# Loads of weight slices that wait one step less, and quantizing two tiles at a time in the first half of a stage

## What is computed

```
x = x + attn(layernorm(x))
x = x + ffn(layernorm(x))

attn: q, k, v = x Wq^T, x Wk^T, x Wv^T     (8 query heads, 2 kv heads, of 256)
      rope on q and k; unit layernorm of q (times 256), k, v per head
      scores q k^T / 16, causal window of 512, 30 tanh(s / 30), softmax, times v, times Wo^T

ffn:  h = relu(bitlinear(x, w1))^2         (w1 is 8192 x 2048)
      y = bitlinear(h, w2)                 (w2 is 2048 x 8192)
bitlinear(x, w): w_scale = 1 / mean|w|;      w_q = clip(round(w * w_scale), -1, 1) / w_scale
                 x_scale = 127 / max|x| per token; x_q = clip(round(x * x_scale), -128, 127) / x_scale
                 return x_q w_q^T
```

## Time and profile before

| | us |
|---|---|
| runs | 7140.6 and 7159.1, median 7149.9 |
| the profiled execution | 7127.2 |
| its span on the slowest core | 7125.6 |
| spans of the 8 cores | 7056.1 to 7125.6 |

### The profile page before, as it was taken

How to read it: one execution, slowest core, us unless ns; L and a number is a source line. 1 busy time by engine, 2 the same in 40 slices (tenths; PEclk the granted TensorE clock), 3 DMA queues, 4 the chain that set the end, 5 groups by cost and what they waited for, 6 DMA issues and landing times.

```text
span 7125.6 us, 37166 instructions; the slowest of 8 cores (7056.1 to 7125.6 us)
## 1 busy us (share of the span) xinstructions
PE 3207.2 (45%) x12168; PEld 1280.3 (18%) x12168; DVE 2700.4 (38%) x2542; ACT 1311.1 (18%) x1432; POOL 372.3 (5%) x516
## 2 busy tenths in 40 slices
PE   0153254243435253166665555551454644655543
PEld 0021022111112111022222222220221211222211
DVE  2233335243444445233334444443443533433312
ACT  1232332221213040233333333321000000000000
POOL 1000000000000000000000000000000000000000
PEclk9676677676768677588888777775777877877776
DMA  8333331402020201655554444433577777777766
GB/s 178 124 112 112 113 99 37 83 30 59 15 68 6 67 11 50 139 165 165 165 165 145 161 154 157 145 133 127 153 169 157 152 141 144 152 152 156 158 183 194
DMA packets 447711, 872.30 MB, mean 122 GB/s; under 512 B 280608, under 2 KB 301088, under 8 KB 393760
## 3 DMA queue, kind: packets, MB, share of 16 engines
q0 software_dynamic: 81920, 457.21, 26.2%
q1 hardware_dynamic: 232480, 379.16, 16.5%
q10 hardware_dynamic: 133120, 33.56, 3.4%
HBM read 491.29 MB, written 334.50 MB: 116 GB/s over the span
## 4 chain that ended last, share of the span: by engine, by line
DMA 38%; DVE 21%; ACT 11%; PE 8%; ACTq 8%; issue 6%; SPq 4%; DVEq 4%; POOLq 0%; PEldq 0%
DMA yacc_hbm<-arena_f 13%; DMA h_hbm<-arena_f 5%; ACTq L186 5%; DMA arena_f<-w2T 4%; DVEq L212 4%; SPq L186 4%; DMA arena_f<-w1T 4%; DVE arena_f L1118 3%; DMA arena_f<-x_tm 3%; PE ps_o L777 3%; ACTq L212 3%; DMA w2q_hbm<-arena_bf 2%; DMA arena_f<-h_hbm 2%; DMA arena_f<-x_hbm 2%; ACT arena_bf L927 2%
## 5 line engine op out<-in xcount | busy, mean ns | idle before, releaser
L1106 PE MATMUL ps<-arena_bf 128*128 128x512 bf16 x4096 | 1071.1, 428 | 1148.4 <-DMA arena_bf<-hq_hbm 683.9
L996 PE MATMUL ps_f<-arena_bf 128*128 128x512 bf16 x4096 | 1102.9, 437 | 891.0 <-DVE arena_f L1003 735.6
L1106 PEld LDWEIGHTS ps<-arena_bf 128*128 128x128 bf16 x4096 | 433.8, 108 | 1785.7 <-issue 1426.4
L996 PEld LDWEIGHTS ps_f<-arena_bf 128*128 128x128 bf16 x4096 | 438.7, 109 | 1554.7 <-issue 1215.3
L1118 DVE COPY arena_f<-ps 128x2048 f32<-128x2048 f32 x128 | 293.2, 2291 | 982.2 <-POOLq L1131 541.6
L777 PE MATMUL ps_o<-arena_bf 128*128 128x512 bf16 x1024 | 267.7, 421 | 361.1 <-DVE arena_f L787 339.7
L551 PE MATMUL ps_k<-arena_bf 128*128 128x512 bf16 x320 | 85.3, 428 | 691.1 <-DMA arena_bf<-xn_hbm 670.9
L719 DVE TENSOR_TENSOR arena_f<-arena_f,arena_bf 128x1024 f32<-128x1024 f32 x128 | 156.8, 1225 | 497.2 <-ACT arena_f L713 487.5
L1003 DVE TENSOR_SCALAR arena_f<-ps_f,fac 128x1024 f32<-128x1024 f32 x128 | 163.7, 1279 | 357.8 <-DMA h_hbm<-arena_f 349.1
L551 PE MATMUL ps_q<-arena_bf 128*128 128x512 bf16 x1024 | 238.0, 396 | 128.0 <-ACT arena_bf L566 128.0
L182 POOL DMA_DIRECT2D arena_f<-w1T x128 | 108.8, 852 | 3436.8 <-SPq L198 1600.4
(11 more groups left out here) (112 smaller groups left out, 3444.8 us busy)
## 6 DMA issues: line engine op xcount, KB each, us to landing
arena_f<-w1T POOLq DMA_DIRECT2D x128, 1024.0 KB, 8.8
arena_f<-w2T POOLq DMA_DIRECT2D x128, 1024.0 KB, 10.8
yacc_hbm<-arena_f POOLq DMA_DIRECT2D x128, 1024.0 KB, 9.1
h_hbm<-arena_f SPq DMA_DIRECT2D x128, 512.0 KB, 3.4
arena_f<-h_hbm SPq DMA_DIRECT2D x128, 512.0 KB, 7.0
arena_f<-x_tm SPq DMA_DIRECT2D x36, 1024.0 KB, 5.9
w2q_hbm<-arena_bf SPq DMA_DIRECT2D x64, 512.0 KB, 2.6
arena_bf<-w2q_hbm POOLq DMA_DIRECT2D x64, 512.0 KB, 11.8
```

What stands on the lines that cost most here:

```text
L996: e.matmul(ps_f[tb][:, nb * 512:(nb + 1) * 512], l, r, start=(kc == 0), stop=(kc == 15)),
L1106: e.matmul(ps3[tb][:, nb * 512:(nb + 1) * 512], l, r, start=(kc == 0), stop=(kc == 7)),
```

## The change

In phase 1b, the load of slice i waits for the count of finished abs to be one lower than before: for abs i-2, the last one that read the same buffer. In phase 3, the 16 quantizings for the next stage are issued two at a time within tiles 0 to 7, and none within tiles 8 to 15. They keep their order and their place within a tile: after the tile's matmuls, ahead of its eviction in VectorE's order. The number of instructions and transfers is the same.

```diff
                 def w1_mean_slice(i):
                     rc, qt = i // 4, i % 4
                     pb = i % 2
-                    w = [("w1ab_done", P.val("w1ab_done"))] if i >= 2 else []
+                    w = [("w1ab_done", max(0, P.val("w1ab_done") - 1))] if i >= 2 else []
                     ld = P.dma("gpsimd", w1p[pb][:],
...
-                        if sc + 1 < NSC:
-                            quant_hq(sc + 1, tc)
+                        if sc + 1 < NSC and tc < 8:
+                            quant_hq(sc + 1, 2 * tc)
+                            quant_hq(sc + 1, 2 * tc + 1)
                         eb = 0
```

## The result

| | before | changed |
|---|---|---|
| median of the runs, us | 7156.6 (10 runs, 7124.0 to 7196.1) | 7275.4 (11 runs, 7256.7 to 7292.2) |
| ratio | | 1.0166, 95% interval 1.0143 to 1.0188 |
| span of the profiled execution, slowest core | 7125.6 | 7281.0 |
| the same, median of the 8 cores | 7091.1 | 7254.1 |

The change costs 119 us, 1.7%: more than the 31 forecast, and still under 2% here (beside other runs of the kernel before, on two other chips, it costs 132 us, 1.9%, and 162 us, 2.2%: see the experiments). It lies inside the stated range. The profiled execution of before took 7127 us against a median of 7157, that of the changed kernel 7283 against 7275, so the two traces differ by 155 us where the medians differ by 119.

What follows compares the result with a forecast made beforehand. No engine fills the span; waits and chains bind: w1 slices in phase 1b, quantizing or accumulates in phase 3. Slices -141, paired quantizing +172 give +31 us: 7158 from the profiled 7127, 7181 from the runs' median 7150; range 7070 to 7320.

Steps and rivals of the forecast that it cites:

- part 1, 12 chunks: Phase 1b: earlier w1 slice loads save 12.2 us in each of 12 chunks, 146 us.
- part 1, the transpose windows: Phase 1b: one more 1 MB load in each of three xn transpose windows, some 2 us each, 5 us lost.
- stage 0, pairs: Phase 3, stage 0: seven intervals with two quantizings take 17.76 instead of 8.88 us, +62 us.
- stage 0, the rest of its tiles and the gap: Phase 3, stage 0: other intervals +1 us; gap to stage 1 falls from 60.9 to 37.5, -23 us.
- stages 1 to 6, pairs (each): Phase 3: seven intervals with two quantizings take 18.5 instead of 12.3 us, +43 us a stage.
- stages 1 to 6, the later intervals (each): Phase 3: seven intervals without quantizing, up to eviction 14, take 10.9 us, -10 us a stage.
- stages 1 to 6, eviction 14 to the next first (each): Phase 3: transposes start one interval earlier; this stretch falls from 77.1 to 65.9 us, 11 saved a stage.
- sum of stages 1 to 6: Phase 3: longer first halves, shorter second halves and gaps make +22 us a stage, +132 for six.
- The first rival: Phase 3: both h loads of two quantizings pay 7.8 us, period 24.9; sum +301 us, 7451; chance 0.11.
- L1106's waits for hq largely replaced by waits for w2q: Phase 3, TensorE at stage starts: a sign the forecast is right, w2q's load being late next; no size given.
- The second rival: Phase 3 gaps: transposes slow what they move onto by as much as they come earlier; +120 us, 7270; chance 0.12.
- The 15.4 us: Phase 3, gap after stage 0: w2q loads alone take 15.4 us, last issue after 3.6, then 11.8 to landing.

Runs made afterwards that it cites:

- p2_ahead: Kernel before with only the paired quantizings, plus the next h load written ahead of the hq store in SyncE's queue: 7065.7 us, ratio 0.9945.
- p2_whq: Kernel before with only the paired quantizings, plus the transposes' wait on g_hqfree let go by one stage: 7357.5 us, ratio 1.0364.
- best_nopairs: As `best`, but with one quantizing in each of the 16 tiles as in the kernel before: 6872.8 us, ratio 0.9672.
- best: Changed kernel plus h loads ahead of stores, g_hqfree wait let go by one stage, w2q loads spread over tiles 7 to 14: 6806.7 us, ratio 0.9580.
- part 2 alone: Kernel before with only the phase 3 change, quantizings two at a time in tiles 0 to 7: 7340.3 us (1.0400), repeated 7330.6 (1.0314).
- p1_late: Kernel before with only the earlier w1 slice loads, keeping the old wait for each group's first chunk: 6963.2 us, ratio 0.9799.

## Why the prediction was right, and where it was off

Both that the change stays within 2%, on this chip, and the range held; its number was 88 us short in the medians (+31 forecast, +119 measured) and 132 in the traces' median core (+163). By its steps, in us, worked out as in the tables above:

| step | forecast | measured |
|---|---|---|
| part 1, 12 chunks | -146 | -143 |
| part 1, the transpose windows | +5 | +45 |
| stage 0, pairs | +62 | +61 |
| stage 0, the rest of its tiles and the gap | -22 | -20 |
| stages 1 to 6, pairs (each) | +43 | +45 |
| stages 1 to 6, the later intervals (each) | -10 | -7 |
| stages 1 to 6, eviction 14 to the next first (each) | -11 | -4 |
| sum of stages 1 to 6 | +132 | +208 |
| phases 1c and 2, stage 7, the rest | 0 | +12 |

- *Pairs.* Right, in mechanism and size: a period of 18.5 was forecast from 4.57 us of VectorE and issue, a load of 4.2 and one of 5.0; the traces have 18.7, and the pair shown 4.0 and 5.1. The first rival (both loads at 7.8) is out. `p2_ahead` shows that the exposed load is the cause of most of it.
- *Stage 0.* +40 forecast, +41 measured.
- *Part 1's chunks.* Right: 31 us forecast for a chunk, 32 measured. TensorE and VectorE bind no chunk.
- *The transpose windows, "some 2 us each".* The step that failed in part 1. I priced one more megabyte; what happened is that two loads at once stretch the issue of 16 transposes, by 12 us in the opening shown and by 41 in the three on the median core. Undoing the burst gave back 15 to 23 us of the 30 to 39 that the openings had lost.
- *The gap of stages 1 to 6, "Saved 11".* The step that failed in part 2, worth 44 of the 76 us missing there. That the wait on g_hqfree holds the transposes back was right (`p2_whq` lets it go and they move). The sizes were not. For before I had 77.1 us from eviction 14 on, worked out for the slowest core; as the mean of all cores it is 72.0, and that is 5 of the 7 us. For the changed kernel I had eviction 15 after 22.5 us and the next first after 43.4 more; it was 16.4 and 52.0. I held that w2q's load would end last, with transposes of their old length. In six of the seven gaps TensorE waited for hq instead. Over all cores and stages 2 to 7 the eight transposes start 13 us earlier than before, measured from eviction 14, but take 55.5 us to issue instead of 46.7 (68 in the rows above), so their end moves by 4 us only, and the first eviction follows it by 12 to 13 us in both kernels. What stretches them can be read from the other traces: 34.3 us in `best_nopairs`, where w2q's loads are spread over earlier tiles; 46.7 before, with one accumulate and w2q's loads over them; 47.0 in `p2_whq`, beside three accumulates; 55.5 with two accumulates and w2q's loads. The sign "L1106's waits for hq largely replaced by waits for w2q" therefore failed, with 587.5 us for hq and 33.1 for w2q. The second rival ("the gaps give nothing back") was nearer for these stages. That its 7270 stands beside a measured 7275 is partly chance: stage 0's gap did give back its 22 us, and the windows' 40 us were in no rival.
- *The later intervals, 10.9.* They came at 11.4, mean of stages 1 to 6.
- *Readings.* The earlier trace rows are called "alone", but SyncE's queue had issued a load of h at 4890.68, half a microsecond ahead of them. The 15.4 us taken from them served all the same: stage 0's gap was forecast at 37.5 us and came at 35.1.

The Trainium skill's rule on queues sharing the 16 engines ("DMA: Bandwidth & Descriptors", "Issuing engines are not separate DMA queues") was named beside that rival. The trace agrees that the moved work is not free: 17 us in for 19 us out in `p2_whq`, 20 for 40 in `best` against `p2_ahead`. The rule of 2.0 us plus bytes at 436 GB/s (the Trainium skill, "DMA: Bandwidth & Descriptors", "Anatomy of one DMA") would have made the 12 chunks about 161 us; they show the row's side of it (143 measured, 146 forecast).

What stays open: why the openings keep 15 us of part 1's loss when the burst is gone (7 of them are in the transposes, and nothing was run on the rest); why the kernel before took 7059 us on one chip and 7157 on another, while part 2 alone took 7340 and 7331 on two; and what the kernel before gains from its h loads issued ahead of the stores with nothing else changed, which would say what a pair costs once its load is hidden.

## What to carry to other kernels

Before moving work to where there seems to be room, look at what its loads wait for: work that hides its load behind another engine's step is cheap one at a time and exposed two at a time. A wait lowered by one does nothing when the instruction stands behind another wait in its queue; read the queue's timeline after the edit, not the semaphore's name. And transfers taken out of a gap come back in part in the intervals they are moved to, even where the DMA engines are only 0.57 busy: 17 of 19 us for the transposes alone, 20 of 40 with w2q's loads. Count both, and expect the difference, not the gap.

## What the runs showed of the hardware

- Sixteen transposing loads were issued in 24.9 us with three 1 MB loads spaced 10 us apart beside them, and in 36.6 us with two of these at once and a third 7 us later (core 2, one opening). Per opening, on the median core, it was 24 to 26 us before, 38 to 41 in the changed kernel, and 26 to 29 in `p1_late`.
- Eight transposing loads (of hq, stages 2 to 7, means over stages and cores, in brackets the shortest and longest) took 34 us to issue beside one accumulate (27 to 49, `best_nopairs`), 47 with w2q's eight loads over them as well (36 to 61, before), 47 beside accumulates alone (35 to 68, `p2_whq`), and 56 beside accumulates and w2q's loads (41 to 79, the changed kernel).
- The kernel before took 7059, 7101, 7101 and 7157 us (medians) in four comparisons. Part 2 alone took 7340 and 7331 us in two of these, where before took 7059 and 7101. A difference of 40 us between two kernels can so be the chip's, unless both run on the same one.
